# Two depthwise convolutions on one core: contiguous bands, and a second copy of the gathered high rows made by VectorE

## What is computed

```python
# x: (8, 384, 128, 128) fp32
x = x + dwconv3x3(gn(x), k)                 # pad 1, one 3x3 filter per channel
w_sym = (w + rot90(w) + rot180(w) + rot270(w)) * 0.25
x = x + dwconv7x7(gn(x), w_sym)             # pad 3, one 7x7 filter per channel
# gn: 32 groups of 12 channels, mean and variance over the 12 channels and the image
```

## Time and profile before

| what | value |
|---|---|
| median of three executions | 3462.82 us (3456.75 to 3474.27) |
| profiled execution | 3465.62 us, of which the span is 3463.8 us |
| busy: TensorE, VectorE, ScalarE, GpSimd | 84%, 66%, 63%, 45% of the span |
| mean granted TensorE clock | 0.937 |
| 16 DMA engines, share of 200 to 3300 us | 0.90 |

### The profile page before, as it was taken

The page is one execution under the profiler, slowest core; times in us unless marked ns, Lnnn a source line. Parts: engine busy times, 40 slices in busy tenths (PEclk is TensorE's granted clock), DMA queues, the critical chain, the costliest instruction groups (busy, mean ns, idle before and its releaser), DMA issues.

```text
span 3463.8 us, 75946 instructions
## 1 busy us (share of the span) xinstructions
PE 2905.4 (84%) x28676; PEld 1702.8 (49%) x28676; DVE 2290.0 (66%) x4988; ACT 2185.6 (63%) x3969; POOL 1550.5 (45%) x1552
## 2 busy tenths in 40 slices
PE   0568888889888889989888988888988888898895
PEld 0235555455545555555454555555555555555453
DVE  3646666667666667666666666666766666767663
ACT  1436666667666667666666666666766666766672
POOL 3334444454444445444444444444444444544442
PEclk9889999999999999999999999999999999999998
DMA  7898899998889989898888898998989988988876
GB/s 123 193 239 246 253 256 258 254 255 250 254 249 257 251 254 259 252 256 256 249 252 249 249 254 252 258 253 253 251 254 256 255 251 251 262 255 259 249 224 191
DMA packets 1081095, 852.26 MB, mean 246 GB/s; under 512 B 204344, under 2 KB 990776, under 8 KB 1080664
## 3 DMA queue, kind: packets, MB, share of 16 engines
q1 hardware_dynamic: 675224, 646.03, 67.7%
q10 hardware_dynamic: 405504, 201.38, 20.4%
HBM read 262.32 MB, written 221.88 MB: 140 GB/s over the span
## 4 chain that ended last, share of the span: by engine, by line
PE 83%; issue 12%; SPq 3%; DVE 1%; DMA 1%
PE PS L685 43%; PE PS L713 39%; SPq L234 2%; PE PS L650 1%; PE PS L657 1%; DVE X L359 0%; DMA rows<-v_all 0%; SPq L225 0%; DMA v_all<-BT 0%; DMA BAND<-rows 0%; DMA BT<-H 0%; DVE X L479 0%; DMA v_all<-X 0%; DVE BT L374 0%; SPq L209 0%
## 5 line engine op out<-in xcount | busy, mean ns | idle before, releaser
L713 PE MATMUL PS<-BT,BAND 126*32 126x512 f16 x21504 | 1342.7, 410 | 436.5 <-issue 426.7
L685 PE MATMUL PS<-H,BAND 128*128 128x512 f16 x6912 | 1548.1, 383 | 61.2 <-DMA BAND<-rows 54.5
L614 POOL TENSOR_TENSOR H<-Z,H 128x512 f16<-128x512 f32 x768 | 846.5, 1103 | 1251.5 <-ACT Z L526 1250.2
L713 PEld LDWEIGHTS PS<-BT,BAND 126*32 126x32 f16 x21504 | 825.8, 133 | 949.2 <-issue 656.7
L685 PEld LDWEIGHTS PS<-H,BAND 128*128 128x128 f16 x6912 | 858.1, 126 | 700.4 <-DMA BAND<-rows 54.6
L606 POOL TENSOR_SCALAR H<-X,RB 128x512 f16<-128x512 f32 x768 | 679.0, 902 | 616.0 <-DVE RB L419 417.3
L523 ACT ACTIVATE H<-X,RB 128x512 f16<-128x512 f32 x768 | 618.0, 805 | 185.3 <-DVE H L452 175.8
L506 ACT ACTIVATE Z<-X,RB 128x512 f32<-128x512 f32 x768 | 561.3, 801 | 94.7 <-DVE RB L419 83.7
L526 ACT ACTIVATE Z<-X,RB 128x512 f32<-128x512 f32 x768 | 615.0, 801 | 0.0
L549 ACT ACTIVATE DUMP<-X 128x512 bf16<-128x512 f32 x768 | 479.7, 625 | 150.3 <-DVE X L479 150.0
L452 DVE TENSOR_TENSOR H<-Z,H 128x512 f16<-128x512 f32 x768 | 535.5, 752 | 47.4 <-POOL H L606 45.1
(11 more groups left out here) (45 smaller groups left out, 365.9 us busy)
## 6 DMA issues: line engine op xcount, KB each, us to landing
BT<-H SPq DMA_DIRECT2D x1152, 174.6 KB
X<-in_x SPq DMA_DIRECT2D x768, 256.0 KB, 4.2
out_y<-X ACTq DMA_DIRECT2D x768, 256.0 KB, 4.8
BT<-H SPq DMA_DIRECT2D x1152, 149.6 KB
BAND<-rows SPq DMA_DIRECT2D x96, 220.5 KB
rows<-v_all SPq DMA_DIRECT2D x8, 1764.0 KB, 11.5
BAND<-rows SPq DMA_DIRECT2D x192, 51.0 KB, 3.3
BAND<-rows SPq DMA_DIRECT2D x192, 49.5 KB, 3.8
```

The costliest lines, as they stand in the source:

```text
L614: g.tensor_tensor(part(H1, n, 1, img, O1, P1), Z[:, img, :].rearrange("p (c w) -> p c w", c=CC), part(H1, n, 0, img, O1, P1), ALU.subtract ...
L685: last = mm(PA[:, ch, :], band[:, j, ws, :], data[:, :, O1 - 1 + j:O1 - 1 + j + W], start=k == 0, stop=k == 3 * K1 - 1)
L713: last = mm(banks2(n)[b * BL:(b + 1) * BL, ch, :], band[:, j, :], rows, start=j == 0, stop=j == K2 - 1, tile_position=(0, b * BL))
```

## The change

Conv 2's window shrinks from 42 to 39 rows for the inner blocks (halo 5 to 4). `BT` is no longer interleaved: partitions 0 to 38 hold the high rows, 64 to 102 the high rows again, and the low rows stand in what is left, the first 24 at 40 to 63 and the last 15 at 103 to 117. So a matmul of conv 2 contracts over 118 rows. The high rows are gathered once (4 DMAs), the low rows in two pieces per block (8 DMAs). The second copy of the high rows is one VectorE instruction at the end of its slot: 39 partitions x 8512 fp16 elements, from partitions 0 to 38 to partitions 64 to 102, which first waits for the 4 high DMAs. TensorE's conv 2 waits for the low DMAs and for this copy. The bands are stored row by row in HBM, so that a row of 4 (conv 1) or 12 (conv 2) channels is one contiguous run: 1584 or 1632 bytes and 5376 bytes. `BAND1` still takes 4 DMAs per step, `BAND2` 4 per group instead of 3. `cut1(1, G)` has 93 x 32 pieces of 1632 bytes instead of 372 x 32 of 408. `BAND2` is cleared once at the start by GpSimd.

```diff
-WIN = 42
-HALO = 5
+WIN = 39
+HALO = 4
...
+AGAIN = 64
+SPLIT = 24
+LOW1 = AGAIN - SPLIT
+LOW2 = AGAIN + WIN
+KW = LOW2 + WIN - SPLIT
+HIGH_LANDED = 16 * NB
+LOW_LANDED = 16 * NB * 2
...
-                sp.dma_start(rows1[g0 * GC:g1 * GC],
-                             bass.AP(v1_all.tensor, g0 * GC * V1 + (Q - 1) * 2 * K1,
-                                     [[V1, (g1 - g0) * GC], [-2 * K1, Q], [1, R1]])).then_inc(rows1_cut[g0 > 0], 16)
+                sp.dma_start(rows1[g0 * CPU_:g1 * CPU_],
+                             bass.AP(v1_all.tensor, g0 * GC * V1 + (Q - 1) * CC * 2 * K1,
+                                     [[CC * V1, (g1 - g0) * CPU_], [-CC * 2 * K1, Q], [1, CC * R1]])
+                             ).then_inc(rows1_cut[g0 > 0], 16)
...
-            def gather(n, k):
-
-                q, which = n % 2, (0, 1, 0)[k]
+            def gather_high(n):
+
+                q = n % 2
                 for b in (0, 2, 1, 3):
                     lo_row, hi_row, r0 = window(b)
-                    first = TERMS * r0 + k
-                    sp.dma_start(BT[first:first + TERMS * (hi_row - lo_row - 1) + 1:TERMS, q, b, :, :],
-                                 H2[lo_row:hi_row, q, which, :, :]).then_inc(gathered[q], 16)
+                    sp.dma_start(BT[r0:r0 + hi_row - lo_row, q, b, :, :],
+                                 H2[lo_row:hi_row, q, 0, :, :]).then_inc(high_gathered[q], 16)
+
+            def gather_low(n):
+
+                q = n % 2
+                for b in (0, 2, 1, 3):
+                    lo_row, hi_row, r0 = window(b)
+                    at1, at2 = LOW1 + r0, LOW2
+                    middle = lo_row + SPLIT - r0
+                    sp.dma_start(BT[at1:at1 + middle - lo_row, q, b, :, :],
+                                 H2[lo_row:middle, q, 1, :, :]).then_inc(low_gathered[q], 16)
+                    sp.dma_start(BT[at2:at2 + hi_row - middle, q, b, :, :],
+                                 H2[middle:hi_row, q, 1, :, :]).then_inc(low_gathered[q], 16)
...
-                        k0 = (m0 - (q * Q - 1)) * 2 * K1
-                        sp.dma_start(BAND1[q * Q:(q + 1) * Q, c * CC:(c + 1) * CC, m0 * 2 * K1:m1 * 2 * K1],
-                                     rows1[bass.ds(g * GC + c * CC, CC), :, k0:k0 + (m1 - m0) * 2 * K1]
-                                     .rearrange("c r k -> r c k")).then_inc(band1_loaded[c], 16)
+                        k0 = (m0 - (q * Q - 1)) * CC * 2 * K1
+                        sp.dma_start(BAND1[q * Q:(q + 1) * Q, c, m0 * CC * 2 * K1:m1 * CC * 2 * K1],
+                                     rows1[g * CPU_ + c, :, k0:k0 + (m1 - m0) * CC * 2 * K1]
+                                     ).then_inc(band1_loaded[c], 16)
...
                     wait_apart(sp, hi_done[1], NI * at(n) + NI)
-                    gather(n, 0)
-                    gather(n, 2)
+                    gather_high(n)
                     wait_apart(sp, lo_done[1], NI * at(n) + NI)
-                    gather(n, 1)
+                    gather_low(n)
...
+                n = t - 3
+                if real(n):
+                    dve.wait_ge(high_gathered[n % 2], ((at(n) - n % 2) // 2 + 1) * HIGH_LANDED)
+                    v.tensor_copy(BT[AGAIN:AGAIN + WIN, n % 2, :, :, :].rearrange("p b c l -> p (b c l)"),
+                                  BT[0:WIN, n % 2, :, :, :].rearrange("p b c l -> p (b c l)")).then_inc(high_again, 1)
                 if t > NCH:
                     add_conv2(t - 5, at)
```

More of the change, by code:

```diff
@@ L132, in conv_program @@
         stored = [sem(f"stored{r}") for r in range(BODY)]
-        gathered = [sem(f"gathered{q}") for q in range(2)]
+        high_gathered = [sem(f"high_gathered{q}") for q in range(2)]
+        low_gathered = [sem(f"low_gathered{q}") for q in range(2)]
+        high_again = sem("high_again")
         rows1_cut = [sem("rows1_cut_first"), sem("rows1_cut_rest")]
@@ L201, in cut1 @@
             def cut1(g0, g1):
[L203 to L205 removed]
+                sp.dma_start(rows1[g0 * CPU_:g1 * CPU_],
+                             bass.AP(v1_all.tensor, g0 * GC * V1 + (Q - 1) * CC * 2 * K1,
+                                     [[CC * V1, (g1 - g0) * CPU_], [-CC * 2 * K1, Q], [1, CC * R1]])
+                             ).then_inc(rows1_cut[g0 > 0], 16)
             def cut2(g0, g1):
[L209 removed]
+                first = rows2[0:1, g0:g0 + 1, :]
+                sp.dma_start(bass.AP(rows2.tensor, first.offset,
+                                     [[B2, (g1 - g0) * 2 * GC], [G * 2 * GC * B2, WIN], [1, B2]]),
                              bass.AP(v2_all.tensor, g0 * 2 * GC * V2 + (WIN - 1) * K2,
@@ L270, in slot @@
                         wait_apart(sp, conv2_done, at(n) - GCH)
[L271 to L274, removed]
+                    for to, r0, r1, which in ((0, 0, WIN, 0), (AGAIN, 0, WIN, 1), (LOW1, 0, SPLIT, 0),
+                                              (LOW2, SPLIT, WIN, 0)):
+                        sp.dma_start(BAND2[to:to + r1 - r0, half, :, :].rearrange("r c k -> r (c k)"),
+                                     rows2[r0:r1, g, which * GC * B2:(which + 1) * GC * B2]
+                                     ).then_inc(band2_loaded[half], 16)
                 if 0 < t < G // CUT:
@@ L366, in prepare @@
                 if layer == 0:
-                    rows = [(v1v[:, :, Q + 1 - dy, :, 0], v1v[:, :, Q + 1 - dy, :, 1], w1v[:, :, dy, :])
+                    rows = [(v1v[:, :, Q + 1 - dy, :, :, 0], v1v[:, :, Q + 1 - dy, :, :, 1], w1v[:, :, :, dy, :])
                             for dy in range(K1)]
                 else:
-                    rows = [(v2v[:, 0, :, WIN - K1 - dy, :], v2v[:, 1, :, WIN - K1 - dy, :], sq(wt)[:, :, dy, :])
+                    rows = [(v2v[:, 0, :, WIN + 2 - HALO - dy, :], v2v[:, 1, :, WIN + 2 - HALO - dy, :], sq(wt)[:, :, dy, :])
                             for dy in range(K2)]
@@ L593, in _ @@
                 g.memset(flat32(whole), 0.0).then_inc(zeroed, 1)
-            for whole in (H2[:], v2_sb):
+            for whole in (H2[:], v2_sb, BAND2[:]):
                 g.memset(flat32(whole), 0.0).then_inc(zeroed, 1)
-            pool.wait_ge(zeroed, 11)
+            pool.wait_ge(zeroed, 12)
             def high_parts2(n, at):
@@ L602, in high_parts2 @@
                 if n >= 2:
-                    wait_apart(pool, gathered[n % 2], ((at(n) - n % 2) // 2) * LANDED)
+                    wait_apart(pool, high_gathered[n % 2], ((at(n) - n % 2) // 2) * HIGH_LANDED)
+                    wait_apart(pool, low_gathered[n % 2], ((at(n) - n % 2) // 2) * LOW_LANDED)
                 rb = RB[:, 1, (n // CPU_) % 2]
@@ L679, in slot @@
                         copied(t, at)
-                    band = BAND1[:, c * CC + ch, :].rearrange("p (m j s) -> p j s m", m=P, j=K1)
+                    band = BAND1[:, c, :].rearrange("p (m k j s) -> p k j s m", m=P, k=CC, j=K1)[:, ch]
                     k = 0
@@ L695, in slot @@
                     half = (n // GCH) % 2
-                    pe.wait_ge(band2_loaded[half], (at(n - n % BODY) // BODY + 1) * (16 * TERMS))
-                    pe.wait_ge(gathered[n % 2], ((at(n) - n % 2) // 2 + 1) * LANDED)
+                    pe.wait_ge(band2_loaded[half], (at(n - n % BODY) // BODY + 1) * 64)
+                    pe.wait_ge(low_gathered[n % 2], ((at(n) - n % 2) // 2 + 1) * LOW_LANDED)
+                    pe.wait_ge(high_again, at(n) + 1)
                     if n == NCH - CONV2:
```

14 lines of the change are left out of this document (6 added, 8 removed).

## The result

The changed kernel took 3436.68 us (median of 6, 3427.77 to 3442.19) beside 3463.36 us (6 runs) for the kernel before on the same chip: a ratio of 0.9898, interval 0.9877 to 0.9918. So it is 1.0% faster, inside the range, where 4.8% was forecast. The profiled span is 3435.3 us.

What follows compares the result with a forecast made beforehand. TensorE, when fed, was taken to bound the kernel before, VectorE the changed one. 180 steady slots from 17.03 to 15.9 us gave -203 us, the start +36: span 3463.8 to 3297, time 3296 us; range 3050 to 3510.

Steps and rivals of the forecast that it cites:

- The spreading rule: On the DMA queues: a DMA is spread over the largest number up to 16 that divides its rows.
- the wait ahead of the copy: On VectorE before the copy: waits for GpSimd of 1.6, 1.5 and about 0.2 us, 3.3 us per three slots.
- VectorE stands still for the high rows: Rival: VectorE waits 8.7 us for the high gathers, 18.2 us per slot, 3716 us; 9 in 100.
- Its counterargument: On SyncE: twelve gathers issued in 9.1 instead of 13.2 us, so the next slot's gathers start some 5 us earlier.
- the port wait: VectorE's copy held by GpSimd's instructions: 1.6 and 1.5 us in two slots of three, about 0.2 in the third.
- four near-equal limits (14.3, 14.45, 14.6, 14.8): Per slot in us: fullest DMA engines 14.3, TensorE 14.45, SyncE's issuing 14.6, VectorE's work without waits 14.8.
- the same twelve gathers take as long to issue as now: Rival: SyncE caused the 13.2 us of gather issuing; slots stay at 17.03 us, 3500 us; 14 in 100.
- the forecast's signs of being wrong: Unheld copies of 4 us, several-us high-row waits, 17 us slots with SyncE unpaused, or first conv 1 beyond 200 us.
- 236 ns: On the DMA engines: time of one gathered row of 4256 bytes, giving 5.7 us per slot for 24 rows.
- the row of the start: A small VectorE operation took 16.38 us at the start, ending with GpSimd's last clearing; taken as VectorE being kept out.
- +36 us forecast: At the start: the second cut of conv 1's bands on three engines, 992 pieces each at 90.5 ns, 90 us.
- the forecast's own case: VectorE bounds at 15.9 us per slot, 3296 us; slots 15.2 to 16.6, start 0 to +60 us; 55 in 100.

Runs made afterwards that it cites:

- base: The changed kernel itself, without further edits, against the kernel before: 3436.7 us, ratio 0.9898.
- three_blocks: The changed kernel with three gathers per block and no VectorE copy, the three terms one behind the other in BT: 3542.8 us, ratio 1.0228 to the kernel before.
- three_spread: The changed kernel with the old three gathers per block, interleaved in BT, and no VectorE copy: 3441.6 us, ratio 0.9921 to the kernel before.
- low_on_act: The changed kernel with the second piece of the low rows, 4 of 12 gathers per step, issued by ScalarE: 3351.2 us, ratio 0.9666 to the kernel before.

## Why the forecast was right in sign and wrong in size

**Right.** The spreading rule and the count of packets held: share of the DMA engines 0.82 from 400 to 3200 us (0.90 before), near the 80% said. The copy took 2.37 us at its least and 2.419 in the mean, against 2.38. The 118 rows of contraction changed nothing: a matmul of conv 2 takes 382 ns at the median before and after. SyncE issued for 14.5 us per slot from 400 to 3200 us (15.9 before), against 14.6.

**The step that failed: the wait ahead of the copy.** The forecast put 3.3 us per three slots there, for GpSimd's series, and nothing for the DMAs. It measured the reverse: 455.1 / 64 = 7.1 us per three slots for the high rows, and next to nothing for GpSimd (the longest copy is 3.05 us, the mean 0.05 above the least). From 400 to 3200 us VectorE is busy 2345.6 us, 42.3 us per three slots. With 6.5 for the high rows (steps 15 to 184; 7.1 is the mean with start and end) and 1.7 for all other waits that is the 50.5 us that three slots took, where the forecast had 47.7. Its 44.4 us for work had some 2 us of waits in it.

**Why the high rows came too late.** The rival "VectorE stands still for the high rows" named this place, with 9 in 100, and gave 8.7 us of standing if SyncE does not get earlier and 6.0 us per three slots as the point from which nothing is left. Its counterargument was that SyncE would begin some 5 us earlier. That came true. Over steps 15 to 184 SyncE began the four high gathers 1.5 us before VectorE was through with y in the kernel before, and 8.0 us before in base. What was wrong is the conclusion. By the forecast's own figures 8.7 - 5 leaves 3.7 us, more than the port wait that it set against them, and the two terms behind the 8.7 were short: the four took 4.4 us to issue, not 3.2, and the last landed some 4.7 us after its issue (median where VectorE waited), not 3.7. So 9.1 us are needed and 8.0 were there in the mean. It also looked at one slot of three. In slots t % 3 = 0 the lead is 5.6 us and VectorE stands 4.1 us; in the other two the leads are 8.7 and 9.6 us, and it stands 1.9 and 0.5.

**Why it reaches the slot.** The forecast read four near-equal limits (14.3, 14.45, 14.6, 14.8) as separate bounds, of which the largest counts. The runs fit one loop better: high rows issued and landed, copy, `finish`, `add_conv2`, low parts, low rows issued, bands, loads, high rows of the next step. Three changes of its links, each by itself, reached the slot in part: 1.42 us more issuing gave 0.68, 2.2 us less copying gave 0.57, four gathers fewer on SyncE gave 0.51. Against the kernel before, slots t % 3 = 1 got shorter (20.1 to 17.5 us from one conv 1 to the next) and slots t % 3 = 2 longer (15.7 to 18.2). The rival "the same twelve gathers take as long to issue as now", 14 in 100, was right about the gathers: 0.91 us each in the mean before and 0.92 in base. The 1.4 us that the queue gained per slot came from bands and loads. A piece of 12 rows costs about as much to issue as one of 36 (0.71 us at the median against 0.74 for the first high one of a slot):

```profile
L235 SPq DMA_DIRECT2D BT<-H x768: 714/806/2999, 177.4 to 3402.0; - x192
```

```profile
L245 SPq DMA_DIRECT2D BT<-H x768: 727/734/2570, 180.8 to 3414.1; - x192
```

```profile
L247 SPq DMA_DIRECT2D BT<-H x768: 548/801/2408, 181.5 to 3414.9; - x192
```

So fewer rows in the same twelve DMAs bought the queue nothing on its gathers, and splitting the low rows spent the one issue per block that the high rows had saved. Of the forecast's signs of being wrong, a wait of several us for the high rows came in full, and slots of 17 us with hardly a pause of SyncE came nearly.

**The price of a gathered row.** 236 ns were carried over from before; it is 288 in base. 24 rows per slot on the fullest engines are then 6.9 us, not 5.7. three_blocks against three_spread shows that the place of the destination can do such a thing: 270 against 222 ns, and 3% of the time with 36 rows. How much of base's loss it is was not separated.

**GpSimd.** The forecast went by the row of the start, where VectorE stood through four GpSimd instructions, against the rule of the Trainium skill ("SBUF — State Buffer", section "Who interferes with whom") that the first to issue holds the shared ports for one instruction. Here the rule was the better guide: in base 60 of 192 copies began inside a series and ten of these took over 2.7 us, in low_on_act 88 and three. The cost is GpSimd's, 2.2 us onto the series, so onto the high parts.

**The start.** +36 us forecast, +20 measured (first conv 1 at 105.3 instead of 85.5 us): three engines as said, but at most 73 ns per piece and engine instead of 90.5 (72 us over 992 pieces). The first twelve slots, which the forecast left as they were, then took 236.9 us instead of 250.4 and gave 13.5 us back. Why was not tried.

**What was luck.** The measured time lies inside the range of the forecast's own case, 3130 to 3450, but the slot of 16.84 us lies outside its 15.2 to 16.6. The milder start and the first twelve slots brought the time back in.

## What to carry over

Limits that lie close together can be links of one loop as soon as work waits on them in order, and then no single one of them gives the time. A new wait also brings a new deadline: the high rows were needed for conv 2 and are now needed 10 us sooner (an estimate: the conv 1 of 8 us ahead of it, and the copy's 2.4), which a mean per engine does not show. Price such a wait in every slot of the pattern, as the last landing less the moment at which the engine is free. Count the DMAs on a queue, not their rows: the time to issue a gather did not fall with its size. Before a DMA's outer dimension is changed, look at its divisors: with 93 rows instead of 372 the first conv 1 came 20 us later, and cutting them in 48 and 45 brought it 57 us forward.

## What the runs showed of the hardware

- In base a gather from SBUF to SBUF takes 0.71 to 0.81 us to issue whether it has 12, 24 or 39 rows; with 16 rows it takes 0.56 (medians by place in the slot; the fourth of the slot, at 1.07 us with 36 rows, is the exception). Loads of bands from HBM take 0.42 us when each partition's share is one run, and took 0.80 when it was four.
- The same SBUF gathers take 22% longer per row when their destinations are adjacent partitions (270 ns in three_blocks against 222 in three_spread).
- An fp16 copy of 39 x 8512 elements on VectorE takes 2.37 us. It can start in the middle of a GpSimd series and lengthens it by about its own duration (5.24 us instead of 3.02, low_on_act).
- A VectorE operation did stand for 16.38 us behind GpSimd's clearings at the start, and in base, with one clearing more, for 18.46 us. Why the copy is let in between pieces of line 635 and that one was not stays open; the clearings write only.
